# Linear attention and feed-forward block: small matmuls in one group, scores a slot ahead of their AV, A doubled, projections in the scores' PSUM banks

## The chip, the cores and the metric

One core of a Trainium2 chip (trn2) runs the whole program. The metric is the device time of one execution in microseconds (us); smaller is better. The figure for the kernel before is the median of three executions.

## The reference

The input x has 8 batches of 2048 tokens with 512 features, all fp32. With 16 heads of 32 features:

```
q = exp(x @ Wq.T + bq); k = exp(x @ Wk.T + bk); v = x @ Wv.T + bv     # split into heads
kv = cumsum over tokens of k (outer) v;  k1 = cumsum over tokens of k
attention = (q . kv) / (q . k1)
x1 = layernorm(x + attention @ Wo.T + bo)
out = layernorm(x1 + tanh(x1 @ weight @ aux_weight1 @ aux_weight2 + bias))
```

The cumulative sums make it a causal linear attention: inside a tile of 128 tokens it is computed as scores, a triangular mask and a product with v (AV below), and what lies before the tile comes from a running state of k (outer) v for each batch.

## The kernel before

**Tiles and slots.** The work is cut into 128 tiles of 128 tokens. Tile n belongs to batch n mod 8, so that the eight batches advance side by side and a batch's state is needed again only eight tiles later. Each of the five engines runs its own program of slots, and each slot k does that engine's share of several tiles at different stages; `run_slots` unrolls slots -8 to 7, then has a loop over the middle, and unrolls the last 16 and some that drain the pipeline. Semaphores tie the engines together. Within an engine the order is written out by hand and is kept: an instruction that waits holds up all behind it.

**Large matmuls.** Each of the five 512x512 products (the projections of q, k and v, the output projection `oproj`, the feed-forward `ffn`) is done as 12 matmuls of 128x128 by 128x512 (`three_pass`, L310 to L312): every fp32 operand is held as a high part of type fp32r and a rest, H and L, and H.H + H.L + L.H is summed for each of 4 blocks of rows. That is 60 large matmuls a slot. The three weight products of the feed-forward are multiplied into one during the setup.

**Small matmuls.** Scores (L367, 32 instructions a slot), denominator `den` (L390, 32), state times q `num` (L395, 32, from tile 8 on), AV (L402, 32) and state update (L414, 32, not for the last eight tiles). They use parts of the array: 32x128, 32x32, 32x32, 128x32 and 128x32 (rows x columns).

**TensorE's order in slot k.** scores(k), v(k), oproj(k-1), then den(k), num(k), AV(k), state(k-1), then q(k+4), k(k+4), ffn(k-2). Scores(k) wait for o(k-1) (L681), since `SC` holds the scores first and then numerator and denominator. The last four slots with scores have no q and k projections.

**PSUM.** `SC` has four banks. G0 to G3 are one bank each: state and k projection, oproj and ffn, q projection, v.

**VectorE's order in slot k.** z = ffn + bias for tile k-3 (L626); four scans for the sum of k (L632), a copy of their last column (L637) and the product with q (L640), all for tile k; transposes of x1 (L645, tile k-2), of k (L648) and of x (L655, tile k+8); second layernorm's statistics (L658, L661, tile k-3); r = x + oproj for tile k-1 (L665) and its statistics (L667, L669); state update (L673); reciprocal (L679) and multiplication (L681) for o(k).

**ScalarE's order in slot k.** Scores from PSUM to `A` (L501, four), tanh(k-3) (L506), V (L511), the high part of x (L516) and of x1 (L523), x1 = normalised r(k-1) (L530), exp for q (L535), second normalisation (L540), high part of o (L545), exp for k (L549).

**GpSimd's order in slot k.** Mask on `A` (L700, four), y = tanh + x1 (L707), the low part of x (L713) and of x1 (L718), the three small steps of layernorm 1 (L722 to L727) and of layernorm 2 (L731 to L736), x + constant (L742), the low part of o (L746).

**DMA queue (SyncE).** x1 is turned from rows to columns by a store to DRAM (L283), four loads (L287) and a transpose on VectorE in 32x32 blocks; k likewise (L275, L278). L271 loads x, L294 loads it again for the residual, L298 stores the result.

Of the kernel before, what the change touches and what calls it, by code (L numbers as in the profile page):

```python
# [26 lines left out]
def linear_attention_ffn_kernel(nc, x, wqT, wkT, wvT, woT, bq, bk, bv, bo, w, a1T, a2, bf, out):  # L27
    F32 = mybir.dt.float32
# [28 lines left out]
    with ctx:  # L57
# [17 lines left out]
        A = sb("A", [P, HG, NK, P])  # L75
# [32 lines left out]
        state_ps, kproj_ps = G[0], G[0]  # L108
        oproj_ps, ffn_ps = G[1], G[1]
        qproj_ps = G[2]  # L110
        v_ps = G[3]

# [40 lines left out]
        a1T_raw = A[:, :, :, :].rearrange("p h g q -> p h (g q)")  # L153
# [77 lines left out]
        def _(sp):  # L231
# [33 lines left out]
            def slot(c, k):  # L265
                if c.exists(k + 9):
# [6 lines left out]
                if c.updates_state(k):  # L273
                    wait_before(sp, (k_turned, c.count(k + 1)))
                    sp.dma_start(k_rows, KS).then_inc(k_stored[k % B], 16)  # L275
                    wait_before(sp, (k_stored[k % B], c.dma_count(k)), (state_done, c.count(k)))
                    for j in range(HG):
                        sp.dma_start(Ktok[j * HD:(j + 1) * HD, :].rearrange("p (a c) -> p a c", a=HG),  # L278
                                     k_blocks[j]).then_inc(ktok_loaded[k % B], 16)
                n = k - 1  # L280
                if c.exists(n):
                    wait_before(sp, (x1_ready, c.count(k)))
                    sp.dma_start(x1_rows, x1[:, n % 2, :]).then_inc(x1_stored[n % B], 16)  # L283
# [5 lines left out]
                if c.exists(k + 1):  # L289
                    if c.static() and c.it * B + k == -1:  # L290
                        sp.wait_ge(c_done, 1)
                    wait_before(sp, (x1_ready, c.count(k)))
                    m = k + 1
                    sp.dma_start(xres[:, m % 2, :], x_t[m % B, c.it + m // B]).then_inc(xres_loaded[m % B], 16)  # L294
# [11 lines left out]
        def _(pe):  # L306
# [8 lines left out]
            def multiply_aux():  # L315
# [3 lines left out]
                for m in range(NK):  # L319
                    cols = slice(m * P, (m + 1) * P)  # L320
                    three_pass(SC[:, m, :], lambda f: a1TH[:, f, cols], lambda f: a1TL[:, f, cols],
                               lambda f: a2H[:, f, :], lambda f: a2L[:, f, :]).then_inc(a12_done, 1)

            def multiply_weight():
# [5 lines left out]
                for m in range(NK):  # L330
                    cols = slice(m * P, (m + 1) * P)
                    three_pass(SC[:, m, :], lambda f: wH[:, f, cols], lambda f: wL[:, f, cols],
                               lambda f: a12H[:, f, :], lambda f: a12L[:, f, :]).then_inc(wf_done, 1)

            def multiply_bv():
# [4 lines left out]
                for k in range(NK):  # L340
                    last = nc.tensor.matmul(SC[:, 0, :], bvrep[:, k, :], wo_raw[:, k, :],
# [5 lines left out]
            def slot(c, k):  # L347
# [3 lines left out]
                cols = slice(b * P, (b + 1) * P)  # L351
                att = c.exists(k)
# [5 lines left out]

                if att:
# [3 lines left out]
                    wait(pe, o_ready, c.count(k))  # L363
# [6 lines left out]
                    if not prev:  # L370
                        pe.wait_ge(wvh_ready, 1)
                        pe.wait_ge(wvl_ready, 1)
                    wait(pe, v_ready, c.count(k))
                    three_pass(v_ps[:, :], lambda f: xTH[:, s, f, cols], lambda f: xTL[:, s, f, cols],
                               lambda f: WvH[:, f, :], lambda f: WvL[:, f, :]).then_inc(v_done, 1)
                if prev:
                    if not c.exists(k - 2):
                        pe.wait_ge(woh_ready, 1)
                        pe.wait_ge(wol_ready, 1)
                    wait(pe, oh_ready, c.count(k))  # L380
                    wait(pe, ol_ready, c.count(k))

                    wait(pe, z_ready, c.count(k - 2))
                    three_pass(oproj_ps[:, :], lambda f: oH[:, f, :], lambda f: oL[:, f, :],
                               lambda f: WoH[:, f, :], lambda f: WoL[:, f, :]).then_inc(oproj_done, 1)
                if att:
                    wait_before(pe, *[(scores_out[j], c.count(k + 1)) for j in range(HG)],
                                (qk1_ready, c.count(k + 1)))
                    for g, j, quarter, h in heads:
                        last = nc.tensor.matmul(den_ps[quarter, j, :], ones[h, :], qk1[h, g, :], start=True, stop=True)  # L390
                    last.then_inc(den_done, 1)
                    if c.reads_state(k):
                        wait_before(pe, (state_ready, c.count(k - 7)))
                        for g, j, quarter, h in heads:
                            nc.tensor.matmul(num_ps[quarter, j, :], state[h, k % B, g, :], QT[h, s, g, cols],  # L395
                                             start=True, stop=False, skip_group_check=True)
# [389 lines left out]
```

## Time and profile before

| | |
|---|---|
| time, median of 3 | 2325.98 us (2323.97 to 2326.26) |
| profiled execution: its own time | 2327.15 us |
| profiled execution: span of the trace | 2325.3 us |
| TensorE busy (matmul) | 2263.8 us, 97% |
| VectorE, ScalarE, GpSimd busy | 1575.0 us, 1024.5 us, 1460.9 us |
| granted TensorE clock, mean | 0.994 |

Times of the trace run from the start of the span, which covers the program's own instructions; the execution's own time is 1.85 us longer. PE is TensorE's matmuls, PEld its weight loads, DVE is VectorE, ACT ScalarE, POOL GpSimd, SPq the queue that issues DMAs. A granted clock of 1.0 is 2.4 GHz, 0.5 is 1.2 GHz. A row of the timeline merges neighbouring instructions of one line of the kernel; x32 says how many there are, and a number in brackets is the idle time of the engine ahead of them with what ended it.

### The profile page before, as it was taken

How to read it: one execution, taken by the hardware profiler on the slowest of the kernel's cores; microseconds unless marked ns; L12 is line 12 of the kernel's file. 1: busy time of each engine (PE TensorE's matmuls, PEld its weight loads, DVE VectorE, ACT ScalarE, POOL GpSimd, SP SyncE). 2: the span in 40 equal slices, each digit the busy share in tenths (PEclk: the TensorE clock that was granted, in tenths of full speed). 3: DMA queues.
4: the chain of work that ended last, by engine and by line, in shares of the span. 5: the costliest groups of instructions: out<-in, count | busy, mean ns of one | idle time of the engine just before them, and what ended most of it. 6: DMA issues, size and time to landing. Idle time of an engine off the chain costs nothing.

```text
span 2325.3 us, 70786 instructions
## 1 busy us (share of the span) xinstructions
PE 2263.8 (97%) x27752; PEld 1824.1 (78%) x27752; DVE 1575.0 (68%) x2316; ACT 1024.5 (44%) x1683; POOL 1460.9 (63%) x1925
## 2 busy tenths in 40 slices
PE   3999999999999999999999999999999999999996
PEld 3788888888888888888888888888888888888874
DVE  3566776776776776776776776776676676676675
ACT  2444444444444444444444444444444444444443
POOL 1266666666666666666666666666666666666565
PEclk9999999999999999999999999999999999999998
DMA  6233333333333333333333333333333333333222
GB/s 160 62 106 109 111 102 110 109 103 107 111 102 109 110 102 106 113 102 108 111 102 107 112 102 109 111 101 106 114 101 108 112 101 107 113 102 109 75 62 67
DMA packets 294451, 242.73 MB, mean 104 GB/s; under 512 B 33328, under 2 KB 225840, under 8 KB 294192
## 3 DMA queue, kind: packets, MB, share of 16 engines
q1 hardware_dynamic: 294192, 238.69, 33.6%
q8 instruction: 234, 3.83, 0.7%
q14 instruction: 25, 0.20, 0.0%
HBM read 139.99 MB, written 98.57 MB: 103 GB/s over the span
## 4 chain that ended last, share of the span: by engine, by line
PE 96%; DVE 1%; DMA 1%; ACT 1%; SPq 0%; POOL 0%; issue 0%; POOLq 0%; DVEq 0%; ACTq 0%
PE G L310 27%; PE G L311 25%; PE G L312 25%; PE SC L367 6%; PE SC L402 6%; PE SC L395 3%; PE SC L390 2%; PE G L414 2%; DVE o L679 1%; PE SC L310 0%; PE SC L312 0%; PE SC L311 0%; DMA KT<-wkT 0%; DMA QT<-wqT 0%; SPq L271 0%
## 5 line engine op out<-in xcount | busy, mean ns | idle before, releaser
L700 POOL TENSOR_SCALAR_AFFINE_SELECT A<-A 128x512 f32<-128x512 f32 x512 | 380.8, 776 | 480.4 <-ACT A L501 480.3
L501 ACT ACTIVATE A<-SC 128x512 f32<-128x512 f32 x512 | 264.3, 605 | 390.8 <-PE SC L367 390.8
L626 DVE TENSOR_TENSOR WK<-G,bfbc 128x512 f32<-128x512 f32 x128 | 88.6, 692 | 505.8 <-PE G L312 505.8
L679 DVE RECIPROCAL o<-SC 128x512 f32<-128x512 f32 x128 | 428.6, 3348 | 2.7 <-PE SC L402 2.4
L530 ACT ACTIVATE WK<-xres,shift,rstd 128x512 f32<-128x512 f32 x128 | 104.4, 816 | 463.7 <-POOL shift L727 463.7
L746 POOL TENSOR_TENSOR oL<-o,oH 128x512 fp32r<-128x512 f32 x128 | 165.7, 1294 | 158.5 <-ACT oH L545 158.5
L310 PE MATMUL G<-xTH,WqH 128*128 128x512 f32 x512 | 214.8, 420 | 27.0 <-POOL xTL L713 27.0
L713 POOL TENSOR_TENSOR xTL<-xin,xTH 128x512 fp32r<-128x512 f32 x128 | 163.2, 1276 | 103.2 <-ACT xTH L516 103.2
L310 PE MATMUL G<-WvH,xTH 128*128 128x512 f32 x512 | 214.2, 418 | 0.0
L632 DVE TENSOR_TENSOR_SCAN WK<-ones,k,KT 128x128 f32<-128x128 f32 x512 | 212.0, 477 | 0.0
L310 PE MATMUL G<-WfH,x1H 128*128 128x512 f32 x512 | 200.9, 392 | 9.2 <-issue 8.4
L310 PE MATMUL G<-xTH,WkH 128*128 128x512 f32 x512 | 200.3, 391 | 6.4 <-DVE WkL L576 6.4
L310 PE MATMUL G<-WoH,oH 128*128 128x512 f32 x512 | 200.3, 391 | 3.3 <-POOL oL L746 3.3
L311 PE MATMUL G<-xTL,WqH 128*128 128x512 f32 x512 | 201.8, 394 | 0.0
L311 PE MATMUL G<-WvL,xTH 128*128 128x512 f32 x512 | 200.8, 392 | 0.0
L312 PE MATMUL G<-xTH,WqL 128*128 128x512 f32 x512 | 200.2, 391 | 0.0
L311 PE MATMUL G<-WfL,x1H 128*128 128x512 f32 x512 | 200.2, 391 | 0.0
L311 PE MATMUL G<-WoL,oH 128*128 128x512 f32 x512 | 200.2, 391 | 0.0
L312 PE MATMUL G<-WoH,oL 128*128 128x512 f32 x512 | 200.1, 391 | 0.0
L312 PE MATMUL G<-WfH,x1L 128*128 128x512 f32 x512 | 200.1, 391 | 0.0
L311 PE MATMUL G<-xTL,WkH 128*128 128x512 f32 x512 | 200.0, 391 | 0.0
L312 PE MATMUL G<-xTH,WkL 128*128 128x512 f32 x512 | 199.9, 391 | 0.0
(100 smaller groups left out, 4962.6 us busy)
## 6 DMA issues: line engine op xcount, KB each, us to landing
xin<-x SPq DMA_DIRECT2D x512, 64.0 KB, 2.5
xres<-x SPq DMA_DIRECT2D x128, 256.0 KB, 2.9
x_rows<-WK SPq DMA_DIRECT2D x128, 256.0 KB, 2.1
WK<-x_rows SPq DMA_DIRECT2D x512, 64.0 KB, 2.0
out<-WK SPq DMA_DIRECT2D x128, 256.0 KB, 3.0
k_rows<-WK SPq DMA_DIRECT2D x120, 256.0 KB, 2.0
WK<-k_rows SPq DMA_DIRECT2D x480, 64.0 KB, 2.0
QT<-wqT SPq DMA_DIRECT2D x4, 256.0 KB, 4.3
```

Of the source, the lines that this page charges most:

```text
L310: nc.tensor.matmul(out, statH(k), movH(k), start=(k == 0), stop=False)
L311: nc.tensor.matmul(out, statH(k), movL(k), start=False, stop=False)
L312: last = nc.tensor.matmul(out, statL(k), movH(k), start=False, stop=(k == NK - 1))
L367: last = nc.tensor.matmul(SC[:, j, g * P:(g + 1) * P], KT[h, s, g, cols], QT[h, s, g, cols], start=True, stop=True)
L402: last = nc.tensor.matmul(num_ps[g * HD:(g + 1) * HD, j, :], V[:, k % 2, f0:f0 + HD], A[:, j, g, :], start=not c.reads_state(k), stop=True ...
L501: nc.scalar.activation(A[:, j, :, :].rearrange("p g q -> p (g q)"), SC[:, j, :], ACT.Copy).then_inc(scores_out[j], 1)
L530: nc.scalar.activation(x1[:, n % 2, :], xres[:, n % 2, :], ACT.Identity, bias=shift[:, 0:1], scale=rstd[:, 0:1]).then_inc(x1_ready, 1)
L632: last = nc.vector.tensor_tensor_scan(qk1[:, g, :], ones[:, 0:1].to_broadcast([P, P]), KT[:, s, g, cols], k1[:, k % B, g:g + 1], ALU.mult, ...
L679: nc.vector.reciprocal(o[:, :, :], den_ps).then_inc(recip_ready, 1)
L700: last = nc.gpsimd.affine_select(out=A[:, j, :, :], in_=A[:, j, :, :], compare_op=ALU.is_ge, fill=0.0, base=0, pattern=[[0, NK], [1, P]], ...
L713: nc.gpsimd.tensor_tensor(halves[1], xin[:, m % XIN, :].rearrange("p (t g q) -> p g t q", t=HG, q=HD), halves[0].bitcast(F32), ALU.subtrac ...
L746: nc.gpsimd.tensor_tensor(oL[:, :, :], o[:, :, :], oH[:, :, :].bitcast(F32), ALU.subtract).then_inc(ol_ready, 1)
```

## The change

- `SC` keeps its four banks for the scores alone, and the five large products use them in turn: q in bank 0, k in 1, v in 2, oproj in 3, ffn in 0 again. A second tensor `ND` of four banks takes numerator, denominator, state update and the setup's products.
- `A` is doubled.
- TensorE's slot k begins with one group of all small matmuls: den(k-1), num(k-1), scores(k), AV(k-1), state(k-2). Then come q(k+4), k(k+4), v(k), oproj(k-1), ffn(k-2). In slots without projections ffn(k-2) stands ahead of oproj(k-1).
- Reciprocal and o belong to tile k-1 now. On VectorE, k's and x's transposes, layernorm 2's statistics, the state update, reciprocal and multiplication come ahead of x1's transpose, the scans and the product with q; r(k-1) and its statistics come last.
- On ScalarE x1(k-2) comes first, then tanh, the copies to `A`, exp for q, the high parts of o and x1, exp for k, the second normalisation, V and the high part of x.
- On GpSimd y comes first, then the masks, layernorm 2, the low part of o, of x1, x + constant, the low part of x, and layernorm 1 last.
- The DMA queue stores x1(k-2) and k(k-1) first, then loads x, then x1's and k's blocks.

```diff
-        A = sb("A", [P, HG, NK, P])
+        A = sb("A", [P, 2, HG, NK, P])
-        G = [ctx.enter_context(nc.psum_tensor(f"G{i}", [P, D], F32)) for i in range(4)]
-        num_ps, den_ps = SC[:, :, 0:P], SC[:, :, P:2 * P]
+        ND = ctx.enter_context(nc.psum_tensor("ND", [P, HG, NK * P], F32))
+        num_ps, den_ps = ND[:, :, 0:P], ND[:, :, P:2 * P]
+        state_ps = ND[:, 0, 2 * P:3 * P]
+        qproj_ps, kproj_ps, v_ps, oproj_ps, ffn_ps = SC[:, 0, :], SC[:, 1, :], SC[:, 2, :], SC[:, 3, :], SC[:, 0, :]
...
# TensorE
+                def output_projection():
+                    wait(pe, oh_ready, c.count(k))
+                    wait(pe, ol_ready, c.count(k))
+                    if att:
+                        wait(pe, scores_out[3], c.count(k + 1))
+                    wait(pe, r_ready, c.count(k - 1))
+                    three_pass(oproj_ps, ...).then_inc(oproj_done, 1)
+                def feed_forward():
+                    wait(pe, x1h_ready, c.count(k - 1))
+                    wait(pe, x1l_ready, c.count(k - 1))
+                    if proj:
+                        wait(pe, q_ready, c.count(k + 5))
+                    elif att:
+                        wait(pe, scores_out[0], c.count(k + 1))
+                    wait(pe, z_ready, c.count(k - 2))
+                    three_pass(ffn_ps, ...).then_inc(ffn_done, 1)
+                if prev:
+                    wait_before(pe, (qk1_ready, c.count(k)), (o_ready, c.count(k - 1)),
+                                (state_ready, c.state_count(k - 2)))
+                    (den, and num where c.reads_state(k - 1), for tile k - 1)
                 if att:
                     wait(pe, k_ready, c.quad_count(k))
                     wait(pe, q_ready, c.quad_count(k))
-                    wait(pe, o_ready, c.count(k))
+                    wait(pe, z_ready, c.count(k - 2))
+                    wait(pe, k_ready, c.count(k + 4))
+                    wait(pe, v_ready, c.count(k))
+                    wait(pe, r_ready, c.count(k - 1))
                     (scores of tile k)
+                if prev:
+                    (AV of tile k - 1, state update of tile k - 2)
...
+                    if att:
+                        wait(pe, scores_out[0], c.count(k + 1))
                     wait(pe, q_ready, c.count(k + 4))
                     (q projection, then k with scores_out[1], then v with scores_out[2])
+                if ffn and not proj:
+                    feed_forward()
+                if prev:
+                    output_projection()
+                if ffn and proj:
+                    feed_forward()
...
# ScalarE, the head of its slot
+                if ffn:
+                    n = k - 2
+                    wait(act, shift1_ready, c.count(n + 1))
+                    wait(act, y_ready, c.count(n - 1))
+                    nc.scalar.activation(x1[:, n % 2, :], xres[:, n % 2, :], ACT.Identity, ...).then_inc(x1_ready, 1)
                 if fin:
                     n = k - 3
                     wait(act, z_ready, c.count(n + 1))
                     nc.scalar.activation(y[:, n % 2, :], y[:, n % 2, :], ACT.Tanh).then_inc(tanh_ready, 1)
                 if att:
                     wait(act, scores_done, c.count(k + 1))
-                    wait(act, num_done, c.count(k))
+                    wait(act, num_done, c.count(k - 1))
...
# VectorE, moved blocks in their new order (z stays first)
+                if c.updates_state(k - 1):   (transpose of k for tile k - 1)
+                if c.exists(k + 8):          (transpose of x)
+                if fin:
+                    wait(dve, y_ready, c.count(k - 2))
+                    nc.vector.bn_stats(bnst[:, 1, :], yf).then_inc(bn2_ready, 1)
+                    (bn_aggr)
+                if c.updates_state(k - 2):   (state update)
+                if prev:
+                    wait(dve, num_done, c.count(k))
+                    nc.vector.reciprocal(o[:, :, :], den_ps).then_inc(recip_ready, 1)
+                    nc.vector.tensor_tensor(o[:, :, :], num_ps, o[:, :, :], ALU.mult).then_inc(o_ready, 1)
+                if c.exists(k - 2):          (transpose of x1)
                 if att:                      (scans, copy, product with q, for tile k)
                 if prev:                     (r for tile k - 1 and its statistics, last)
...
# GpSimd, whole slot in its new order
+                y(k - 3); masks(k); layernorm 2 (k - 3); oL(k - 1); x1L(k - 2);
+                xres(k) + cbc; xTL(k + 8); layernorm 1 (k - 1)
```

Lines in brackets and the last two lines stand for blocks that are moved with their indices changed; their instructions are the same.

## Rows read from the trace of the kernel before

**Rows 1.** Windows (length; busy of PE, PEld, DVE, ACT, POOL; clock; DMA).

```profile
230.00:2230.00 2000.00, 2000.00 (x25165) 1616.45 (x25167) 1384.48 (x2055) 897.93 (x1487) 1303.99 (x1714) 1.00 0.34 106
...
2293.50:2299.00 5.50, 5.44 (x12) 3.80 (x12) 1.47 (x3) 0.63 (x1) 2.46 (x2) 0.50 0.26 84
```

**Rows 2.** Timeline of one steady slot, TensorE (start, length, engine, line, what).

```profile
1209.83 0.39 PE L312 MATMUL G<-WfH,x1L 128*128 128x512 f32 x1
1210.15 1.17 PE L367 MATMUL SC<-QT,KT 32*128 32x128 f32 x32
1211.25 0.50 PE L310 MATMUL G<-WvH,xTH 128*128 128x512 f32 x1
...
1211.59 0.40 PE L311 MATMUL G<-WvL,xTH 128*128 128x512 f32 x1
...
1216.60 0.39 PE L312 MATMUL G<-WoH,oL 128*128 128x512 f32 x1
...
1219.56 0.40 PE L311 MATMUL G<-xTL,WqH 128*128 128x512 f32 x1
```

**Rows 3.** Timeline of the same slot, VectorE and ScalarE.

```profile
1210.26 0.69 DVE L626 TENSOR_TENSOR WK<-G,bfbc 128x512 f32<-128x512 f32 x1 [4.07 <-PE G L312]
1210.86 1.60 DVE L632 TENSOR_TENSOR_SCAN WK<-ones,k,KT 128x128 f32<-128x128 f32 x4
...
1216.41 0.69 DVE L658 BATCH_NORM_STATS2 bnst<-WK 128x6 f32<-128x512 f32 x1 [0.56 <-POOL WK L707]
...
1217.29 0.69 DVE L665 TENSOR_TENSOR xres<-G,xres 128x512 f32<-128x512 f32 x1
...
1219.35 0.29 DVE L673 TENSOR_TENSOR state<-G,state 128x128 f32<-128x128 f32 x1 [0.37 <-PE G L414]
1219.56 3.35 DVE L679 RECIPROCAL o<-SC 128x512 f32<-128x512 f32 x1
...
1220.54 0.82 ACT L530 ACTIVATE WK<-xres,shift,rstd 128x512 f32<-128x512 f32 x1 [3.51 <-POOL shift L727]
...
1222.94 0.69 DVE L681 TENSOR_TENSOR o<-SC,o 128x512 f32<-128x512 f32 x1
```

**Rows 4.** Timeline of the last slots: ScalarE, GpSimd and VectorE.

```profile
2303.64 0.81 ACT L540 ACTIVATE WK<-WK,shift,rstd 128x512 f32<-128x512 f32 x1 [0.56 <-POOL shift L736]
2304.35 0.61 ACT L506 ACTIVATE WK<-WK 128x512 f32<-128x512 f32 x1
2305.05 1.26 POOL L707 TENSOR_TENSOR WK<-WK 128x512 f32<-128x512 f32 x1 [1.45 <-ACT WK L506]
```

**Rows 5.** Timeline of slot 1: VectorE and GpSimd together.

```profile
99.02 1.82 DVE L632 TENSOR_TENSOR_SCAN WK<-ones,k,KT 128x128 f32<-128x128 f32 x2
99.08 1.48 POOL L746 TENSOR_TENSOR oL<-o,oH 128x512 fp32r<-128x512 f32 x1 [2.89 <-ACT oH L545]
...
100.87 0.17 DVE L637 COPY k<-WK 128x4 f32<-128x4 f32 x1
101.08 0.69 DVE L640 TENSOR_TENSOR WK<-WK,QT 128x512 f32<-128x512 f32 x1
```

**Rows 6.** All scans, L632 (shortest/median/longest in ns).

```profile
L632 DVE TENSOR_TENSOR_SCAN WK<-ones,k,KT x512: 455/460/1442, 88.1 to 2281.3; 128x128 f32<-128x128 f32 x171
```

**Rows 7.** Chain of waits: scores of slots 3 and 125.

```profile
130.94 1.10 PE SC L367 x32
...
2252.15 1.17 PE SC L367 x32
```

**Rows 8.** Timeline of the end: oproj(127) after a wait, and r(127).

```profile
2293.56 0.77 PE L310 MATMUL G<-WoH,oH 128*128 128x512 f32 x1 [3.31 <-POOL oL L746]
...
2299.05 0.69 DVE L665 TENSOR_TENSOR xres<-G,xres 128x512 f32<-128x512 f32 x1 [2.37 <-PE G L312]
```

**Rows 9.** DMA issues: KB each and median us to landing.

```profile
x_rows<-WK SPq DMA_DIRECT2D x128, 256.0 KB, 2.1
WK<-x_rows SPq DMA_DIRECT2D x512, 64.0 KB, 2.0
```

More of the change, by code:

```diff
@@ L272, in slot @@
                                      x_b[n % B, c.it + n // B, j]).then_inc(xin_loaded[n % B], 16)
[L273 to L283, printed above, removed]
+                if c.exists(k - 2):
+                    n = k - 2
                     wait_before(sp, (x1_stored[n % B], c.dma_count(n)), (x1l_ready, c.count(n)))
@@ L340, in multiply_bv @@
                 for k in range(NK):
-                    last = nc.tensor.matmul(SC[:, 0, :], bvrep[:, k, :], wo_raw[:, k, :],
+                    last = nc.tensor.matmul(ND[:, 0, :], bvrep[:, k, :], wo_raw[:, k, :],
                                             start=(k == 0), stop=(k == NK - 1))
@@ L369, in slot @@
                     last.then_inc(scores_done, 1)
-                    if not prev:
-                        pe.wait_ge(wvh_ready, 1)
-                        pe.wait_ge(wvl_ready, 1)
+                if prev:
                     wait(pe, v_ready, c.count(k))
[L374 to L396, printed above, removed]
-                    wait(pe, v_ready, c.count(k + 1))
-                    wait(pe, masked, c.count(k + 1))
+                    wait(pe, masked, c.count(k))
                     for j in range(HG):
@@ L695, in slot @@
                 fin = c.exists(k - 3)
-                if att:
-                    for j in range(HG):
-                        wait_before(pool, (scores_out[j], c.count(k + 1)))
-                        last = nc.gpsimd.affine_select(out=A[:, j, :, :], in_=A[:, j, :, :], compare_op=ALU.is_ge,
-                                                       fill=0.0, base=0, pattern=[[0, NK], [1, P]],
-                                                       channel_multiplier=-1)
-                    last.then_inc(masked, 1)
                 if fin:
@@ L707, in slot @@
                     nc.gpsimd.tensor_tensor(y[:, n % 2, :], y[:, n % 2, :], x1[:, n % 2, :], ALU.add).then_inc(y_ready, 1)
+                if att:
+                    for j in range(HG):
+                        wait_before(pool, (scores_out[j], c.count(k + 1)))
+                        last = nc.gpsimd.affine_select(out=A[:, k % 2, j, :, :], in_=A[:, k % 2, j, :, :],
+                                                       compare_op=ALU.is_ge, fill=0.0, base=0,
+                                                       pattern=[[0, NK], [1, P]], channel_multiplier=-1)
+                    last.then_inc(masked, 1)
@@ new lines, in slot @@
+                if prev:
+                    wait(pool, oh_ready, c.count(k))
+                    wait(pool, oproj_done, c.count(k - 1))
+                    nc.gpsimd.tensor_tensor(oL[:, :, :], o[:, :, :], oH[:, :, :].bitcast(F32),
+                                            ALU.subtract).then_inc(ol_ready, 1)
+                if ffn:
+                    wait(pool, x1h_ready, c.count(k - 1))
+                    halves = [t[:, :, :].rearrange("p g (t q) -> p g t q", q=HD) for t in (x1H, x1L)]
+                    nc.gpsimd.tensor_tensor(halves[1], x1s[:, :].rearrange("p (t g q) -> p g t q", t=HG, q=HD),
+                                            halves[0].bitcast(F32), ALU.subtract).then_inc(x1l_ready, 1)
```

261 lines of the change are left out of this document (134 added, 127 removed).

## The prediction

> **What bounds the kernel now.** The windows come first: in 2000 us of the middle TensorE is busy for all 2000, at full clock [rows 1]. So the price of a slot is read from TensorE's own order. Large matmuls start 0.2277 us apart (1211.59 to 1216.60 is 22 steps) [rows 2]; 60 of them are 13.66 us. The rest is the two small groups. From the last large start before the scores to the second one after them is 1209.83 to 1211.59, 1.76 us, less two steps 1.30. The group of den, num, AV and state takes 1216.60 to 1219.56, 2.96 us, less two steps 2.50 [rows 2]. Together a slot is 17.46 us, and nothing else is in it. The reader is to see that the other engines are under this bound, VectorE at 1384 and GpSimd at 1304 of 2000 us [rows 1]; but what each waits for, and in which order, will matter below. The chain of waits [rows 7] gives the place of slots 3 (130.94) and 125 (2252.15), so 73.2 us lie behind the scores of slot 125.
>
> **One group instead of two.** The scores cost 1.10 us from their start to the next large start (1210.15 to 1211.25), the other 0.20 of their 1.30 is the way into and out of a group of their own [rows 2]. In the merged group that falls away: 13.66 + 2.50 + 1.10 = 17.26 us. Bounds: nothing gained, if the passage from 32x32 to 32x128 costs as much, or 0.40, if AV's entry vanishes too; I take 0.20, read from the very step that goes. The six waits ahead of the scores, all but z long past, I put at nothing; z comes first from VectorE: 0.43 after the last large start (1209.83 to 1210.26), and 0.69 long [rows 2, 3], so 1.12 after it, where den and num too have just been issued. `A` doubled, the new banks and `ND` change no instruction; bank waits in TensorE's order fall due after L501, which has 1 us of cover in a full slot. Moved transposes, statistics and masks keep their lengths and lie in waits of their engines.
>
> **The loop that the new order closes.** r(k-1) is now last on VectorE, and x1(k-2) first on ScalarE. Follow it: r starts; x1 starts 3.25 later (1217.29 to 1220.54) [rows 3]; tanh, next on ScalarE, 0.71 later; y on GpSimd 0.70 later (2303.64, 2304.35, 2305.05) and 1.26 long [rows 4]; the second statistics, queued behind y on VectorE, 0.03 later (estimate) and 0.88 until what follows both (1216.41 to 1217.29); the state update 0.21 (1219.35 to 1219.56); the reciprocal 3.38 until the multiplication (1219.56 to 1222.94) [rows 3]. That is 10.42 us from r to the multiplication. Behind it stand x1's transpose (starts 0.60 later, as L632 behind L626), the scans (0.60 later), 1.64 for four, 0.21 for the copy (100.87 to 101.08), 0.60 for the product, and then r again [rows 3, 5]: 3.65 us. In all 14.1 us, under 17.26: hidden, if nothing holds up the scans.
>
> **VectorE against GpSimd.** Something does. Now three GpSimd operations in a row (low parts of o and of x1, x + constant), and then the low part of x, start just when the scans do. A scan takes 0.46 us as a rule and 1.44 at the longest [rows 6]; the long one is the second of the two that began at 99.02: it began at about 99.40 and ended at 100.84, and GpSimd's L746 ran from 99.08 to 100.56 [rows 5]. So the pair take turns: GpSimd finishes 1.08 us after the scan ahead of it (scan's end 99.48, 0.46 after 99.02), and the blocked scan ends 0.28 after GpSimd. A round is 1.36 us. Counted from the multiplication's start: oH 0.72 and 0.63 long, oL asks at 1.43; scan 1 ends at 1.68; rounds: oL to 2.76, scan 2 to 3.04, x1L to 4.12, scan 3 to 4.40, x + constant to 5.48, scan 4 to 5.76, the low part of x to 6.84; then copy and product, and r at about 7.5. (0.72, 0.63 and that the copy takes part are estimates from L545's place behind L681 and the copy's 0.42 median beside masks.) The loop is 10.42 + 7.5 = 17.9 to 18.0 us. I take 17.98. Bounds: 17.26, where one round falls away (17.98 - 1.36 is under TensorE's own), and 18.3, if x1's blocks come late too.
>
> The Trainium skill says of this in "SBUF — State Buffer", section "Who interferes with whom", that a VectorE instruction with two SBUF inputs and a GpSimd instruction that reads SBUF exclude each other, and that the first holds the port pair for its whole instruction. The trace agrees that they exclude each other (1.44 against 0.46 us); on the length it gives less than the recorded whole, 1.36 us a round where 1.28 + 0.46 would be 1.74.
>
> **The end.** From slot 124 on there are no q and k to lay over waits, ffn(k-2) stands ahead of oproj(k-1), and oproj is the last thing in the slot; r follows it. ffn needs x1L, which follows oL on GpSimd. So per slot: from the last start of oproj 0.43 to r, 10.42 less the absent state update, 10.2, to the multiplication, 4.12 to x1L's end, 0.12 to TensorE, then 24 large matmuls. The clock: TensorE waited 3.31 us for oL at 2293.56, and in the window from 2293.5 to 2299.0 its granted clock was 0.50, the lower of its two levels (1.2 GHz); 12 matmuls filled it all [rows 1, 8], 5.3 us instead of 2.73. Here it waits longer, some 5 to 8 us in each slot, so ffn runs slow (5.3) and oproj, behind it, mostly fast: 2.8 to its last start. A slot is 0.43 + 10.2 + 4.12 + 0.12 + 5.3 + 2.8 = 23.0 us. All at full clock it is 20.4, all slow 25. The kernel before needs 73.2 us from scores(125) to the end, with five slots in them [rows 7]. After the last r: as now, 2325.3 - 2299.05 = 26.25 [rows 8].
>
> **The sum.** Start: slot 2 holds L501, and q with it, behind x1(0), about 2 us; the merged group gives part back, and slot 3 begins at about 131 (estimate; now its scores are at 130.94). Slots 3 to 123: 121 x 17.98 = 2175.6, less 1.25 of slack that the loop has at first (oL is there 0.8 before TensorE asks), less 0.4 for the last two without a state update: slot 124 begins at 2305.0. Its multiplication is 9.1 later, x1L 4.12, TensorE 0.12, then 5.3 and 2.8: last start of its oproj 2326.4. Four more slots: 92.0, 2418.4. Then 0.43 + 26.25: span 2445. The profiled execution's own time was 1.85 over its span, the median of the runs is 0.7 over it: 2446 us.
>
> **The rivals.**
> *The rounds on the port don't pile up.* The low part of x, or x + constant, may come later, and then scans and copy slip by: one round less and TensorE bounds the slot at 17.26. For it: the low part of x hangs on v's projection and two ScalarE steps, and is due only 0.4 us before it would miss its round. Slot 124 at 131 + 121 x 17.26 = 2219 less 0.6, multiplication at 7.8, the same end (20.1 to the last oproj start, then 92 and 26.7): 2358 us. Chance 24%.
> *Faster.* The end's loop is broken, TensorE in the last five slots finds its operands as now. It decides from there: the merged group gives 113 x 0.20 = 22.6 us less 2.5 for slots 3 to 8, where den alone no longer covers z. That is 2306 us; the other side begins once the end costs under 20 us, 4 a slot. For it: 0.20 us is sure. Against: each step of the end is an in-order queue. Chance 9%.
> *x1's blocks come late.* x1's transpose now stands ahead of the scans. From x1's start: 0.81, store 2.1, four loads issued 1.3 to 1.7 and 2.0 to land [rows 9], after the loads of x in the queue (0.7 to 1.6): 7.0 to 8.2, where the multiplication's way gives 10.42 - 3.25 + 0.6 = 7.8. If it is late by 0.5 in each slot: +60, 2506 us. Chance 6%.
> *The port is held for the whole instruction.* With 1.74 instead of 1.36 for four rounds a slot is 1.5 longer: 2446 + 121 x 1.5 = 2628 us. The page named above gives this rule. Chance 3%.
>
> **How the numbers follow.** The forecast, both loops, has 58%; its own range is 2390 (a slot of 17.5) to 2485 (18.3). The 8 times in 10 are that and the first rival: 2350 to 2485. A time within 0.2%, 4.7 us, is what measurement can't tell from no change. Of the faster case 8% lie beyond it and 1% within; all others are slower: 91%.
>
> **What would show it.** Right: a steady slot of 17.9 to 18.1 us; TensorE idle some 0.7 us a slot, ahead of q (for L501) or of the scores (for z); L632 with a mean near 1 us instead of 0.46; GpSimd's oL, x1L, x + constant and xTL back to back with scans ending in between; at the end slots of about 23 us with the clock at 0.5. Each small group one piece of 3.6 us. Wrong: a steady slot of 17.26 with TensorE never idle (first rival), end slots near 13 (faster), VectorE's L645 waiting for the DMA (third). The steady slot is the step that I trust least: 0.1 us in it is 12 us.

## The result and the profile after

The changed kernel takes 2473.48 us (2469.83 to 2476.86, six executions), the kernel before 2324.97 us on the same chip: 1.0637 times as long, 95% interval 1.0624 to 1.0651. The forecast was 2446 us with a range of 2350 to 2485.

Three stretches of the span, cut at the scores of slots 3 and 125 [rows 7], show where the 148.3 us come from (the span grew from 2325.3 to 2473.6):

| us | before | after | difference |
|---|---|---|---|
| start to scores of slot 3 | 130.9 | 135.5 | +4.6 |
| slot 3 to slot 125, 122 slots | 2121.2 (17.39 each) | 2224.8 (18.24 each) | +103.6 |
| slot 125 to the end | 73.2 | 113.3 | +40.1 |

The middle stretch still contains slot 124, the first slot without q and k projections, which took 22.07 us instead of 13.14. So 8.9 of its 103.6 us belong to the end, and slots 3 to 123 alone took 18.20 us each.

The page of the kernel after: its span, the engines' busy time, the chain that ended last by engine, and two of the costliest groups (busy time and mean ns of one, then idle time ahead of it).

```profile
span 2473.6 us, 71230 instructions
PE 2267.6 (92%) x27784; PEld 1844.8 (75%) x27784; DVE 1935.6 (78%) x2316; ACT 990.4 (40%) x1683; POOL 1432.5 (58%) x1925
DVE 40%; SPq 17%; issue 13%; DMA 9%; PE 8%; POOL 8%; ACT 5%; POOLq 0%; DVEq 0%; ACTq 0%
...
L689 DVE TENSOR_TENSOR_SCAN WK<-ones,k,KT 128x128 f32<-128x128 f32 x512 | 557.2, 1147 | 0.0
...
L524 ACT ACTIVATE WK<-xres,shift,rstd 128x512 f32<-128x512 f32 x128 | 104.2, 814 | 812.8 <-POOL shift L772 812.8
```

The chain of the kernel before, for comparison:

```profile
PE 96%; DVE 1%; DMA 1%; ACT 1%; SPq 0%; POOL 0%; issue 0%; POOLq 0%; DVEq 0%; ACTq 0%
```

TensorE fell from 97% to 92% of the span and from 96% to 8% of the chain; VectorE is now 40% of it. VectorE's program has no additional work, yet it is busy 360 us longer than before (1935.6 against 1575.0): the four scans take 1147 ns each as a mean. The same in the windows of busy time by engine, one in the middle and one at the end (the last three numbers are clock, DMA share and GB/s); they answer to [rows 1]. The second ends 0.7 us behind the slow matmuls that are shown further down, so its clock of 0.53 is a mean with a little of full clock in it.

```profile
240.00:2240.00 2000.00, 1908.26 (x24173) 1558.53 (x24172) 1651.89 (x1973) 830.15 (x1424) 1226.94 (x1647) 1.00 0.33 102
2394.00:2400.00 6.00, 5.97 (x15) 4.72 (x16) 2.43 (x4) 0.00 (x0) 1.29 (x1) 0.53 0.03 9
```

In the middle TensorE now stands still for 92 of 2000 us at full clock.

**A steady slot on TensorE**, the small matmuls (to be read against [rows 2]):

```profile
1206.44 0.39 PE L314 MATMUL SC<-WfH,x1L 128*128 128x512 f32 x1
1206.76 0.50 PE L393 MATMUL ND<-WK,ones 32*32 32x128 f32 x32
1207.08 0.75 PE L397 MATMUL ND<-QT,state 32*32 32x128 f32 x32
1208.44 1.17 PE L410 MATMUL SC<-QT,KT 32*128 32x128 f32 x32 [0.61 <-issue]
1209.55 1.08 PE L419 MATMUL ND<-A,V 128*32 128x128 f32 x32
1210.45 0.48 PE L429 MATMUL ND<-V,WK 128*32 128x32 f32 x32
1211.22 0.47 PE L312 MATMUL SC<-xTH,WqH 128*128 128x512 f32 x1 [0.29 <-ACT A L534]
```

The group is one piece, broken by two waits: ahead of the scores and ahead of q. The profile names nothing for the first; the scores wait for z among others, and z ended at 1208.24, 0.20 before they began. The second is for the copies to `A`. Together the waits are 0.90 us.

**The same slot on VectorE**, from one r to the next, and below it the low parts on GpSimd (compare [rows 3, 5]):

```profile
1205.94 0.68 DVE L702 TENSOR_TENSOR xres<-SC,xres 128x512 f32<-128x512 f32 x1
...
1207.55 0.69 DVE L650 TENSOR_TENSOR WK<-SC,bfbc 128x512 f32<-128x512 f32 x1
...
1211.88 0.69 DVE L664 BATCH_NORM_STATS2 bnst<-WK 128x6 f32<-128x512 f32 x1 [2.42 <-POOL WK L725]
...
1212.93 3.35 DVE L677 RECIPROCAL o<-ND 128x512 f32<-128x512 f32 x1
1216.31 0.69 DVE L679 TENSOR_TENSOR o<-ND,o 128x512 f32<-128x512 f32 x1
1216.92 0.70 DVE L683 STREAM_TRANSPOSE WK<-WK 128x512 f32<-128x512 f32 x1
1217.55 4.56 DVE L689 TENSOR_TENSOR_SCAN WK<-ones,k,KT 128x128 f32<-128x128 f32 x4
1222.14 1.08 DVE L694 COPY k<-WK 128x4 f32<-128x4 f32 x1
1223.25 0.69 DVE L697 TENSOR_TENSOR WK<-WK,QT 128x512 f32<-128x512 f32 x1
1223.86 0.68 DVE L702 TENSOR_TENSOR xres<-SC,xres 128x512 f32<-128x512 f32 x1
```

```profile
1217.75 1.32 POOL L745 TENSOR_TENSOR oL<-o,oH 128x512 fp32r<-128x512 f32 x1 [2.13 <-ACT oH L544]
1219.03 1.42 POOL L750 TENSOR_TENSOR x1L<-WK,x1H 128x512 fp32r<-128x512 f32 x1
1220.42 1.41 POOL L756 TENSOR_TENSOR xres<-xres,cbc 128x512 f32<-128x512 f32 x1
1221.78 1.41 POOL L763 TENSOR_TENSOR xTL<-xin,xTH 128x512 fp32r<-128x512 f32 x1
```

r follows r after 17.92 us: 10.37 to the multiplication, 7.55 from there. Scans and copy fill 1217.55 to 1223.22 while GpSimd's four operations run end to end, 1.28, 1.39 and 1.36 apart. The line's own view gives the single scans of this slot, shortest, median and longest:

```profile
L689 DVE TENSOR_TENSOR_SCAN WK<-ones,k,KT x4: 444/1450/1453, 1217.5 to 1220.7; 128x128 f32<-128x128 f32 x4
```

The first is free (444 ns). The other three, 1450 ns and more, have each waited for a GpSimd operation, and the 128x4 copy too: 1.08 us beside the low part of x, where it took 0.17 in [rows 5].

**Most slots are not like this.** The slot above is one whose x1 blocks came in time. Of the 101 rounds from r(11) to r(112), 29 are of this kind, with a median of 17.93 us from r to r. In 53 VectorE waited for x1's blocks, 0.49 us as a mean, and r followed r after 18.32 us (median). In the other 19 VectorE also stood idle for over 0.5 us ahead of z. The waits of the whole kernel (us in total, times, longest):

```profile
DVE WK L683 <- DMA WK<-x_rows: 50.9, 79, 2.8
DVE WK L650 <- issue: 11.5, 13, 1.0
POOL xres L756 <- DMA xres<-x: 24.5, 61, 0.7
```

Two further pieces of VectorE's timeline, and TensorE's wait that follows the second:

```profile
1235.60 0.71 DVE L683 STREAM_TRANSPOSE WK<-WK 128x512 f32<-128x512 f32 x1 [0.67 <-DMA WK<-x_rows]
...
1244.82 0.69 DVE L650 TENSOR_TENSOR WK<-SC,bfbc 128x512 f32<-128x512 f32 x1 [0.90 <-issue]
```

```profile
1245.71 1.95 PE L410 MATMUL SC<-QT,KT 32*128 32x128 f32 x32 [1.70 <-DVE WK L650]
```

The first is a wait for x1's blocks. The second comes once in eight slots: VectorE starts z 0.90 late with nothing in the profile to wait for. The slot takes 18.9 to 19.4 us (once 20.6) and the next one 17.3 to 17.6, but three times 18.8. Those three include the one shown: behind the 1.70 us of idle time TensorE's granted clock is 0.50, and the scores take 1.95 us instead of 1.17.

The place of these stops is the same each time. The programs' loop over the middle has eight slots a pass and covers slots 8 to 111 in 13 passes; the 13 stops stand at VectorE's first instruction of the 13 passes.

**The end**, a slot's r, multiplication, x1L and TensorE's ffn and oproj (compare [rows 8]):

```profile
2379.62 0.69 DVE L702 TENSOR_TENSOR xres<-SC,xres 128x512 f32<-128x512 f32 x1 [4.56 <-PE SC L314]
...
2389.86 0.69 DVE L679 TENSOR_TENSOR o<-ND,o 128x512 f32<-128x512 f32 x1
```

```profile
2392.55 1.38 POOL L750 TENSOR_TENSOR x1L<-WK,x1H 128x512 fp32r<-128x512 f32 x1
```

```profile
2394.03 0.76 PE L312 MATMUL SC<-WfH,x1H 128*128 128x512 f32 x1 [5.34 <-issue]
2394.59 0.63 PE L313 MATMUL SC<-WfL,x1H 128*128 128x512 f32 x1
...
2399.29 0.56 PE L312 MATMUL SC<-WoH,oH 128*128 128x512 f32 x1
2399.68 0.39 PE L313 MATMUL SC<-WoL,oH 128*128 128x512 f32 x1
```

TensorE idles 5.34 us, then works through ffn at half clock (2394.03 to 2399.29, 5.26 us for twelve matmuls), and comes back to full clock at oproj. Slots 124, 125 and 126 take 22.07, 21.78 and 22.79 us, where they took 13.14 to 13.15.

### The profile page after: what moved, and what is told of

Same layout as the page of the kernel before. It is cut to its first block, busy times and chain, and to the rows that moved or that the text cites. A ratio compares the mean times of both kernels' runs of the same rounds, so it can differ in the third digit from the quotient of the medians.

```text
span 2473.6 us, 71230 instructions
## 1 busy us (share of the span) xinstructions
PE 2267.6 (92%) x27784; PEld 1844.8 (75%) x27784; DVE 1935.6 (78%) x2316; ACT 990.4 (40%) x1683; POOL 1432.5 (58%) x1925
## 4 chain that ended last, share of the span: by engine, by line
DVE 40%; SPq 17%; issue 13%; DMA 9%; PE 8%; POOL 8%; ACT 5%; POOLq 0%; DVEq 0%; ACTq 0%
DVE WK L689 21%; DMA WK<-x_rows 7%; SPq L277 7%; SPq L284 6%; DVE o L677 4%; DVE k L694 4%; DVE bnst L704 4%; DVE xres L702 3%; ACT WK L524 3%; POOL rstd L770 3%; PE SC L312 2%; SPq L271 2%; PE SC L313 2%; PE SC L314 2%; POOL WK L725 2%
## 5 line engine op out<-in xcount | busy, mean ns | idle before, releaser
L689 DVE TENSOR_TENSOR_SCAN WK<-ones,k,KT 128x128 f32<-128x128 f32 x512 | 557.2, 1147 | 0.0
L677 DVE RECIPROCAL o<-ND 128x512 f32<-128x512 f32 x128 | 428.6, 3348 | 10.7 <-PE ND L419 10.7
L664 DVE BATCH_NORM_STATS2 bnst<-WK 128x6 f32<-128x512 f32 x128 | 88.9, 694 | 299.3 <-POOL WK L725 299.3
L534 ACT ACTIVATE A<-SC 128x512 f32<-128x512 f32 x512 | 261.8, 594 | 11.8 <-PE SC L410 11.5
L312 PE MATMUL SC<-xTH,WqH 128*128 128x512 f32 x512 | 211.6, 413 | 56.7 <-ACT A L534 28.9
L312 PE MATMUL SC<-WfH,x1H 128*128 128x512 f32 x512 | 205.3, 401 | 45.9 <-POOL x1L L750 24.6
L312 PE MATMUL SC<-xTH,WkH 128*128 128x512 f32 x512 | 200.3, 391 | 7.3 <-DVE WkL L598 7.3
L313 PE MATMUL SC<-WfL,x1H 128*128 128x512 f32 x512 | 204.2, 399 | 0.0
L314 PE MATMUL SC<-WfH,x1L 128*128 128x512 f32 x512 | 203.9, 398 | 0.0
L314 PE MATMUL SC<-xTH,WqL 128*128 128x512 f32 x512 | 201.9, 394 | 0.0
L313 PE MATMUL SC<-xTL,WqH 128*128 128x512 f32 x512 | 201.4, 393 | 0.0
L313 PE MATMUL SC<-xTL,WkH 128*128 128x512 f32 x512 | 200.1, 391 | 0.0
```

Source lines behind the costliest of these rows:

```text
L312: nc.tensor.matmul(out, statH(k), movH(k), start=(k == 0), stop=False)
L313: nc.tensor.matmul(out, statH(k), movL(k), start=False, stop=False)
L314: last = nc.tensor.matmul(out, statL(k), movH(k), start=False, stop=(k == NK - 1))
L534: nc.scalar.activation(A[:, k % 2, j, :, :].rearrange("p g q -> p (g q)"), SC[:, j, :], ACT.Copy).then_inc(scores_out[j], 1)
L677: nc.vector.reciprocal(o[:, :, :], den_ps).then_inc(recip_ready, 1)
L689: last = nc.vector.tensor_tensor_scan(qk1[:, g, :], ones[:, 0:1].to_broadcast([P, P]), KT[:, s, g, cols], k1[:, k % B, g:g + 1], ALU.mult, ...
```

## The experiments

Each lists what was changed against the kernel after unless said otherwise. The table gives for each the time, its ratio to the kernel before on the same chip, two of the stretches of the span, and the mean length of a scan and of the 128x4 copy.

| kernel | us | ratio (95%) | slots 3 to 125, each | from 125 on | scan ns | copy ns |
|---|---|---|---|---|---|---|
| before | 2324.97 | 1 | 17.39 | 73.2 | 477 | 418 |
| after | 2473.48 | 1.0637 (1.0624 to 1.0651) | 18.24 | 113.3 | 1147 | 794 |
| x + constant early | 2369.24 | 1.0183 (1.0166 to 1.0200) | 17.37 | 112.4 | 861 | 406 |
| x1's blocks first | 2381.76 | 1.0233 (1.0216 to 1.0250) | 17.50 | 113.3 | 947 | 249 |
| oproj first at the end | 2448.65 | 1.0519 (1.0501 to 1.0536) | 18.18 | 94.1 | 1190 | 780 |
| all three and xTL | 2343.22 | 1.0066 (1.0049 to 1.0083) | 17.31 | 94.0 | 912 | 170 |
| reciprocal first at the end | 2334.40 | 1.0037 (1.0023 to 1.0050) | 17.31 | 87.9 | 896 | 170 |
| one more turn | 2600.74 | 1.1185 (1.1168 to 1.1202) | 19.17 | 119.7 | 1213 | 1071 |
| the same in the kernel before | 2328.63 | 1.0009 (1.0000 to 1.0019) | 17.39 | 74.0 | 477 | 420 |
| x1's blocks and residual first | 2448.50 | 1.0531 (1.0515 to 1.0547) | 18.02 | 112.2 | 1214 | 830 |
| x1's transpose behind the scans | 2346.21 | 1.0090 (1.0073 to 1.0107) | 17.39 | 87.4 | 710 | 124 |

**Take a turn out of the loop: x + constant early.** GpSimd adds the constant for tile k-1, a slot later, ahead of the low part of o, where it waits anyway.

```diff
+                if prev:
+                    n = k - 1
+                    (for the first tile: wait for the constant)
+                    wait(pool, xres_loaded[n % B], c.dma_count(n))
+                    nc.gpsimd.tensor_tensor(xres[:, n % 2, :], xres[:, n % 2, :], cbc[:, :],
+                                            ALU.add).then_inc(xb_ready, 1)
                 if prev:
                     (low part of o, low part of x1)
-                if att:
-                    (for the first tile: wait for the constant)
-                    wait(pool, xres_loaded[k], c.dma_count(k))
-                    nc.gpsimd.tensor_tensor(xres[:, k % 2, :], xres[:, k % 2, :], cbc[:, :],
-                                            ALU.add).then_inc(xb_ready, 1)
```

> One edit to the changed kernel: on GpSimd, x + constant for tile k-1 is done in slot k ahead of oL, where GpSimd idles about 2 us, instead of x + constant for tile k behind x1L, where it takes a turn with the scans. Theory A (the steady slot of 17.9 to 18.3 us is a loop r, layernorm 1, x1, tanh, y, statistics 2, reciprocal, transposes, scans, r, lengthened by four turns of VectorE and GpSimd of about 1.38 us each): one turn falls away, scans L689 drop from a mean of 1147 ns to about 800, the loop is about 16.6 us, TensorE binds at 17.3 in most slots, and the time is 2360 to 2390 us. Theory B (the order of r and x1 alone makes the slot, the long scans cost nothing): no change, 2473 us. Theory C (DMA landings of x1's blocks make it): under 10 us gained.

It took 2369.24 us, 104 less than the kernel after for one operation of 1.28 us in another place. The window of the middle:

```profile
240.00:2240.00 2000.00, 1990.65 (x25292) 1631.95 (x25284) 1578.05 (x2063) 883.63 (x1496) 1278.88 (x1730) 1.00 0.34 106
```

TensorE is idle for 9 us of 2000 instead of 92, and most slots are 17.24 us, which is TensorE's own bound. So the loop through the port, and not TensorE, set the pace; and one turn less hands the pace back. The wait for x1's blocks rose in the same run, from 50.9 us in all to this (waits of VectorE: us in total, times, longest):

```profile
DVE WK L683 <- DMA WK<-x_rows: 76.5, 98, 2.8
```

and cost little: with slack in the loop a late block is absorbed.

**The third rival alone: x1's blocks first.** On the DMA queue x1's four block loads are issued ahead of the four loads of x.

```diff
-                if c.exists(k + 9):
-                    (four loads of x)
                 if c.exists(k - 2):
                     (four loads of x1's blocks)
+                if c.exists(k + 9):
+                    (four loads of x)
```

> One edit to the changed kernel: in the DMA queue the four loads of x1's blocks are issued ahead of the four loads of x instead of behind them. The trace of the changed kernel has VectorE waiting 50.9 us in 79 slots for these blocks, and slots of 18.2 to 19.3 us beside those of 17.9. Theory A with late blocks as a second term: those waits go, the slot is 17.9 to 18.0 throughout, 20 to 35 us less, 2440 to 2453 us. Rival (the store's own landing is what is late, or the spread of slots has another reason): under 8 us, 2465 to 2476 us.

It came out at 2381.76 us, 58 us below the low end of what was expected. Waits and groups of this run:

```profile
POOL xres L756 <- DMA xres<-x: 208.5, 117, 4.1
```

```profile
L694 DVE COPY k<-WK 128x4 f32<-128x4 f32 x128 | 31.9, 249 | 4.4
```

The residual's load, last in the queue, now lands after GpSimd asks for it: 208.5 us of waits instead of 24.5. x + constant and the low part of x therefore start after scans and copy have passed (the copy is back to 249 ns), and turns fall away. This is the first rival's mechanism, brought about by a late transfer. That reading was put to a test of its own.

**The same with the residual's load in front too** (the cut is against the kernel just described).

```diff
                 if c.exists(k - 2):
                     (four loads of x1's blocks)
+                if c.exists(k):
+                    (load of the residual)
                 if c.exists(k + 9):
                     (four loads of x)
                 (four loads of k's blocks)
-                if c.exists(k):
-                    (load of the residual)
```

> The changed kernel with the loads of x1's blocks and then the residual's load ahead of the loads of x. In the run with x1's blocks alone ahead, the residual landed later and GpSimd's x + constant waited for it 208 us, until after the scans. Here it lands early again. Theory (late blocks cost about 0.26 us a slot, and what the other run gained beyond that was turns that fell away): all four turns are there, scans L689 at a mean of 1100 to 1200 ns, slots of 17.9 us throughout, 2436 to 2452 us. Rival (the earlier loads themselves gave the 92 us): about 2382 us.

2448.5 us, as expected: the turns are back (scan 1214, copy 830 ns), and the blocks come in time but for 26 slots:

```profile
DVE WK L683 <- DMA WK<-x_rows: 18.1, 26, 2.6
```

The middle is 18.02 us a slot instead of 18.24, and the commonest slot is now 17.9 us. Late blocks had cost 0.21 us a slot, 25 us in all. The other 67 of the 92 us that the run before had gained went with the turns that fell away.

**The end: oproj ahead of ffn in the last slots.**

```diff
-                if ffn and not proj:
-                    feed_forward()
                 if prev:
                     output_projection()
-                if ffn and proj:
+                if ffn:
                     feed_forward()
```

> One edit to the changed kernel: in the last slots, which have no q and k projections, oproj(k-1) stands ahead of ffn(k-2), as it does in all other slots. Theory (the end's slots of 22 us are one chain in which ffn waits for x1L, oproj for ffn, and r for oproj): ffn's 12 matmuls, slow after the wait, and x1L leave the chain; a slot at the end is 16 to 19 us instead of 22, and the time is 15 to 28 us less, 2446 to 2459 us. Rival (the chain through oL alone makes them, or the clock falls in two places instead of one): under 8 us.

2448.65 us, as expected; from slot 125 on 94.1 instead of 113.3 us, and slot 124 17.80 instead of 22.07. oproj waits only for oL, and its end lets r start while ffn runs. TensorE's first matmul of oproj in one of these slots:

```profile
2363.22 0.77 PE L312 MATMUL SC<-WoH,oH 128*128 128x512 f32 x1 [3.59 <-issue]
```

The wait is 3.59 instead of 5.34. The slow stretch has moved: it is now oproj's twelve matmuls that follow each other after 0.43 us, and ffn, no longer in the loop, runs at full clock but for its first two.

**All three, and the low part of x at the head of GpSimd's slot** (for tile k+7, ahead of y).

```diff
+                if c.exists(k + 7):
+                    m = k + 7
+                    (low part of x for tile m)
                 (y, masks, layernorm 2, x + constant for tile k - 1, low parts of o and x1)
-                if c.exists(k + 8):
-                    (low part of x for tile k + 8)
```

> The three edits together, and the low part of x for tile k+7 at the head of GpSimd's slot k instead of that for tile k+8 near its end, so that two of the four turns with the scans are gone. Theory: the loop is about 15.2 us, TensorE binds every full slot at 17.26 (the merged group's 3.61 us and 60 large matmuls at 0.2277), 0.20 less than in the kernel before; slot 124 begins at about 2219 us, end slots take 16 to 19 us. 2318 to 2342 us. If the merged group were no shorter than the two groups together, the slot would be 17.46 and the time over 2340 us.

2343.22 us, 1.2 above the expected range. With only oL and x1L left beside the scans the middle is 17.31 us a slot.

**And the reciprocal first at the end.** Against the last kernel: in the slots from 124 on, reciprocal, multiplication and x1's transpose stand ahead of the second layernorm's statistics, and on GpSimd that layernorm's small steps behind the low parts; in slot 2 ScalarE copies the scores before it makes x1(0).

```diff
-                if fin:
-                    (statistics 2)
+                if not last_slots:
+                    statistics2()
                 (state update, reciprocal, multiplication, transpose of x1)
+                if last_slots:
+                    statistics2()
...
-                    (x1 for tile k - 2)
+                if not second_slot:
+                    first_layernorm()
                 (tanh, copies of the scores)
+                if second_slot:
+                    first_layernorm()
```

> The kernel of the four edits together, with two more: in the last slots (no q and k projections) VectorE does reciprocal, multiplication and x1's transpose ahead of the second layernorm's statistics and GpSimd does that layernorm behind the low parts, so that the reciprocal no longer waits for y; and in slot 2 ScalarE copies the scores ahead of x1(0). Theory (the end is a chain through x1, tanh, y and the statistics to the reciprocal): end slots of 17.5 to 18.9 us become about 15, slot 2 loses 1.5 us, together 10 to 16 us less than 2343: 2327 to 2333 us, about as the kernel before. Rival (in the end slots the chain reciprocal, low part of o, oproj alone makes the length): under 4 us less, 2339 or more.

2334.4 us, 9 below the last and 1.4 over the expected range. TensorE still waits in each of the last slots:

```profile
2285.05 0.47 PE L312 MATMUL SC<-WoH,oH 128*128 128x512 f32 x1 [2.58 <-issue]
```

This is the best version found, and it is still 0.37% slower than the kernel before. Against it by stretches: +2.2 us to slot 3 (133.1), -9.6 in the middle (2111.6 against 2121.2), +14.7 from slot 125 on (87.9 against 73.2); together 7.3.

**Price a turn: one more in each kernel.** GpSimd computes the low part of x1 twice, in the kernel after and, separately, in the kernel before.

```diff
                     nc.gpsimd.tensor_tensor(halves[1], x1s[:, :].rearrange(...),
+                                            halves[0].bitcast(F32), ALU.subtract).then_inc(spare_ready, 1)
+                    wait(pool, spare_ready, c.count(k - 1))
+                    nc.gpsimd.tensor_tensor(halves[1], x1s[:, :].rearrange(...),
                                             halves[0].bitcast(F32), ALU.subtract).then_inc(x1l_ready, 1)
```

> The changed kernel with the low part of x1 computed twice on GpSimd, the second over the first: one more operation of 1.3 us between oL and the scans' end, the result unchanged. Theory A (every GpSimd operation of two inputs among the scans is a turn in a loop that bounds the slot): about 1.4 us more in each of some 120 slots, 2600 to 2650 us. Rival (GpSimd and VectorE have slack there, the slot is set elsewhere): GpSimd is busy 58% of the span, so nothing, under 10 us.

> The kernel before with the same addition, the low part of x1 computed twice on GpSimd. There no scan runs beside it and TensorE bounds the slot. Theory A: no change, within 5 us of the kernel before. Rival (GpSimd is near a bound of its own in either order, 1.3 us a slot shows everywhere): up to 150 us more.

In the kernel after it costs 127 us, 2600.74, at the low edge of what was expected; in the kernel before nothing that can be told, 2328.63 against 2326.98, although GpSimd is busier by 150 us in 2000 there:

```profile
240.00:2240.00 2000.00, 2000.00 (x25169) 1616.01 (x25172) 1384.43 (x2050) 883.98 (x1484) 1454.49 (x1831) 1.00 0.34 105
```

The same instruction has two prices: next to nothing where TensorE binds, and 0.94 us a slot where the loop through the port does. That is less than a whole round of 1.36. In the kernel after, one scan a slot as a rule still ran without waiting; here, in the commonest kind of slot (x1's blocks late, from r to r 19.25 us instead of 18.32), all four scans and the copy have waited. In slots without late blocks r follows r after 19.05 us instead of 17.93. Why an added turn shows as 0.9 to 1.1 us and not as 1.36 was not worked out further. The scan and copy groups of the longer kernel:

```profile
L690 DVE TENSOR_TENSOR_SCAN WK<-ones,k,KT 128x128 f32<-128x128 f32 x512 | 590.9, 1213 | 0.0
...
L695 DVE COPY k<-WK 128x4 f32<-128x4 f32 x128 | 137.1, 1071 | 4.4
```

**The last turns: x1's transpose behind the scans.** Against the best version, except in the last slots.

```diff
-                    (transpose of x1)
                 if att:
                     (four scans)
+                    if not last_slots:
+                        (transpose of x1)
                     (copy, product with q)
```

> The previous kernel (end's reciprocal first) with x1's transpose on VectorE behind the four scans instead of ahead of them, except in the last slots. There VectorE still waited 44 us for x1's blocks, and the steady slot was 17.32 us in the mean instead of 17.24. Theory: with some 2 us more time for the blocks those waits go, every steady slot is 17.24, 6 to 10 us less: 2325 to 2329 us, level with the kernel before, because the 0.21 us gained in each of about 112 steady slots (23 us) is given back at the start (about 4) and at the end (about 18). Rival (the longer slots come from elsewhere, or the low part of x1 is now late for the feed-forward): 2334 us or more.

Missed: 2346.21 us, 12 slower than the version that it starts from. The scans did get shorter, 710 instead of 896 ns, but the middle grew from 17.31 to 17.39 us a slot. Most slots stay at 17.24; one in eight, the first of each pass of the loop, takes 17.4 to 18.7. In these slots TensorE stops within q:

```profile
PE SC L313 <- issue: 10.1, 12, 1.2
```

L313 is the second matmul of a block, the first that reads the low part of x, and it stops 12 times for 10.1 us in all, in the first slot of the passes from the second to the thirteenth. But in the slot looked at that low part was complete at 1194.06, and q's first matmul began at 1195.31, its second at 1197.01: the trace shows nothing that it can have waited for. So shorter scans bring nothing more once TensorE binds, and the new loss is a stop whose cause was not found.

## Why the prediction came out as it did

**The mechanism held.** The loop from r back to r, the turns on the port and the end were each found where the prediction put them. 10.42 us were expected from r to the multiplication, and it was 10.37. From there 7.5 were expected, with four rounds of 1.36 and the copy held too; it was 7.55, with GpSimd's starts 1.28 to 1.39 apart. TensorE's own slot of 17.26 was 17.24, seen where the loop does not bind. Runs bear the loop out: one turn less hands the slot to TensorE, one more costs 127 us, and the same one in the kernel before costs nothing that can be told.

**The steady slot did not, as a rule, have the forecast length.** A slot of 17.98 was forecast, and slots without a late block are 17.92. But most slots have one, and the median of slots 8 to 119 is 18.27, outside the 17.9 to 18.1 that the prediction named as its sign of being right. Only with x1's blocks and the residual loaded first is 17.9 the commonest length.

On the copy, the Trainium skill says in "SBUF — State Buffer", section "Who interferes with whom", that a copy can enter a mode that uses both port pairs and then contends with GpSimd. The trace agrees that this copy contends: 1.08 us beside the low part of x, 0.17 us where GpSimd is silent. That one side holds the ports for its whole instruction would, as the prediction reckoned it, have made rounds of 1.74 us and a time of 2628 us; rounds of 1.28 to 1.39 were measured.

**The forecast is 27 us low, by sizes of terms.** By its own steps:

- *Slot 3 begins at about 131.* It began at 135.5, +4.5. The two microseconds for x1(0) ahead of the copies are there (slot 2 is 18.76 instead of 16.89), but none of what the merged group was to give back; and the way to slot 2 is 2.8 us longer, of which the prediction had nothing: the first scores are 1.4 later and slot 0 is 1.4 longer. In the best version, with the copies first, slot 2 was 17.24; slot 0 stayed long.
- *121 x 17.98.* Slots 3 to 123 took 2202.8 us instead of 2174, +29. The undisturbed slot is 0.06 shorter than forecast. What was missing is the third rival, which was given 6% as a loss of 0.5 in each slot and is there in part: blocks late in 79 slots, and 0.21 us a slot (25 us) when most of that is taken away. It should have stood in the sum as a term, since its own estimate, 7.0 to 8.2 against 7.8, straddled the limit. About 0.1 us a slot is left in that run, where 26 late slots and the 13 stops ahead of z remain; a stop there is visible in no row of before, as VectorE waited for TensorE.
- *End slots of 23.0.* They took 22.07, 21.78 and 22.79, and slot 124 to the end 135.3 instead of 140: -4.7. The wait of TensorE was 5.3 us, at the low end of the 5 to 8 expected, and ffn ran at half clock as forecast. That ffn stood in the end's loop is shown by the run with oproj first.

**The rivals.** That the rounds don't pile up (2358 us) did not happen, but it is the right picture of what the change costs without them: with x + constant early the kernel took 2369. It happened by itself when the residual's load came late. *Faster* did not happen in any version tried: even with the loop shortened and the end rearranged the best one is at 1.0037 (1.0023 to 1.0050). The 0.21 us of the merged group (a slot of 17.24 where TensorE binds) would be 23.5 us in slots 9 to 120. Of that 8.7 are lost in longer slots, 5.9 of them in the fifth slot of each pass of the loop (17.7 us as a mean). Slots 3 to 8 take 1.6 us more than before and slot 124 3.5 more, so 9.6 are left in the middle. The slots from 125 on, where o must be made for the tile before, cost 14.7; TensorE's wait for it is seen there, and that this wait makes up all of it is not shown.

**What stays open.** Why an engine stops once in eight slots. The stops keep to fixed places in the loop's pass: VectorE's 13 at its first instruction of a pass, TensorE's 12 in its first slot (with x1's transpose behind the scans), and where GpSimd's slot begins with the low part of x, GpSimd has 13 too, 7.5 us in all, at that first instruction. TensorE's longer fifth slot keeps to its place too. No run changed the loop or the length of its pass, so that the loop is the cause is not shown. Open is also the way to slot 1: in the changed kernels the first scores came at 88.9 to 90.5 us (88.3 before) and slot 0 took 11.4 to 13.1 (11.5 before).

## What to carry to other kernels

Before work is moved, follow the loop that the new order closes, engine by engine, and put each pair of VectorE and GpSimd instructions that would meet on the port into it as alternating turns; the price of a turn was next to nothing while TensorE bound, and 0.94 us a slot, most of a round, as soon as that loop did. A transfer whose estimate straddles its due time belongs in the sum as a fraction, not among the unlikely rivals, and a late one can also help by moving a contender out of the way. A saving per slot of 1% must be weighed against the last few slots, where no other work covers a longer chain.

## What the hardware showed unexpectedly

Even the 128x4 copy took a turn: 0.17 us free, 1.08 us beside a GpSimd subtraction; over all 128 slots its mean went from 170 ns with nothing beside it to 1071 with one more GpSimd operation. In the slot shown, alternating turns of a 128x128 scan and a 128x512 GpSimd operation came every 1.28 to 1.39 us. After a wait of 5.3 us TensorE ran twelve large matmuls at the lower of its two levels, 0.43 us apart instead of 0.23, and returned to the upper one at the next product. And 13 stops of about 0.9 us stood at VectorE's first instruction of the loop's 13 passes; no row shows them where VectorE waits for TensorE at that place.
